# Where two subtractions that split x into bf16 parts are issued: on GpSimd between its gathers, or on VectorE around the first keys

## The reference

```
def _mp_layer(x, src, dst, edge_attr, W, b):
    # self loops with a zero attribute are appended: src2, dst2, ea2
    msg = concat([x[dst2], x[src2], ea2], axis=1) @ W + b
    agg = segment_sum(msg, dst2, num_segments=n)
    return relu(agg)

h   = relu(_mp_layer(x, src, dst, edge_attr, W1, b1))       # 64 -> 128
out = log_softmax(_mp_layer(h, src, dst, edge_attr, W2, b2))  # 128 -> 64
x   = layernorm(x + out)
```

## Time and profile before

| | us |
|---|---|
| median of three executions (251.25 to 252.3) | 251.34 |
| span of the profiled execution, first to last instruction | 251.8 |
| busy PE | 202.7 (81%), 2089 matmuls |
| busy PEld | 183.9 (73%) |
| busy DVE | 180.2 (72%), 436 instructions |
| busy POOL | 165.0 (66%), 338 instructions |
| busy ACT | 115.1 (46%), 235 instructions |
| chain of waits that ended last | PE 42%, POOL 34%, DVE 12%, DMA 5%, issue 4%, ACT 1% |
| mean granted TensorE clock | 0.972 of full |

### The profile page before, as it was taken

How to read it: one execution, slowest core, us unless ns; L and a number is a source line. 1 busy time by engine, 2 the same in 40 slices (tenths; PEclk the granted TensorE clock), 3 DMA queues, 4 the chain that set the end, 5 groups by cost and what they waited for, 6 DMA issues and landing times.

```text
span 251.8 us, 5544 instructions
## 1 busy us (share of the span) xinstructions
PE 202.7 (81%) x2089; PEld 183.9 (73%) x2089; DVE 180.2 (72%) x436; ACT 115.1 (46%) x235; POOL 165.0 (66%) x338
## 2 busy tenths in 40 slices
PE   1001269599998999989999899989999999999940
PEld 0000159489887898879888798878888999999930
DVE  4035999979876899768977789768410285899881
ACT  2020173267766676757766776667741010101110
POOL 5728998619999999999999999999846000000000
PEclk9999999779999999999999999999999999999995
DMA  1543200000000000000000000000000001010000
GB/s 35 136 115 85 63 21 21 0 3 1 3 2 3 0 3 3 1 3 1 3 1 3 0 3 0 4 0 5 0 3 0 3 3 31 3 31 23 19 15 18
DMA packets 12578, 4.18 MB, mean 17 GB/s; under 512 B 11911, under 2 KB 12126, under 8 KB 12551
## 3 DMA queue, kind: packets, MB, share of 16 engines
q1 hardware_dynamic: 10711, 1.77, 4.0%
q0 software_dynamic: 1840, 2.04, 3.0%
HBM read 2.98 MB, written 0.81 MB: 15 GB/s over the span
## 4 chain that ended last, share of the span: by engine, by line
PE 42%; POOL 34%; DVE 12%; DMA 5%; issue 4%; ACT 1%; POOLq 0%; ACTq 0%; DVEq 0%
PE pset L834 21%; PE acc L826 9%; PE pset L801 5%; POOL u L378 4%; POOL deg L377 4%; DMA adj<-in_dst,adj 4%; POOL t L390 3%; DVE ohl L504 3%; POOL t L394 3%; POOL z L389 3%; POOL u L381 3%; POOL zr L392 3%; POOL base L400 2%; POOL z L398 2%; POOL z L396 2%
## 5 line engine op out<-in xcount | busy, mean ns | idle before, releaser
L715 ACT ACTIVATE adj<-pset 125x1000 bf16<-125x1000 f32 x75 | 77.3, 1032 | 7.0 <-PE pset L801 7.0
L826 PE MATMUL acc<-x,adj 125*125 125x195 bf16 x625 | 75.7, 260 | 2.2 <-POOL x L329 2.2
L504 DVE TENSOR_TENSOR ohl<-iota,keyl 128x1000 bf16<-128x1000 bf16 (+1 forms) x75 | 60.0, 800 | 12.6 <-PE dense L814 11.8
L801 PE MATMUL pset<-ohr,ohl 128*125 128x125 bf16 x600 | 60.0, 255 | 6.0 <-DVE ohr L504 6.0
L826 PEld LDWEIGHTS acc<-x,adj 125*125 125x125 bf16 x625 | 59.7, 143 | 5.7 <-POOL x L329 2.4
L504 DVE TENSOR_TENSOR ohr<-iota,keyr 128x1000 bf16<-128x1000 bf16 (+1 forms) x75 | 60.7, 810 | 0.0
L801 PEld LDWEIGHTS pset<-ohr,ohl 128*125 128x125 bf16 x600 | 50.8, 154 | 7.9 <-DVE ohr L504 6.3
L834 PE MATMUL pset<-z,adj 125*125 125x192 bf16 x625 | 52.8, 247 | 0.0
L834 PEld LDWEIGHTS pset<-z,adj 125*125 125x125 bf16 x625 | 51.7, 136 | 0.3
L529 DVE TENSOR_REDUCE s_sum<-acc 125x65 f32<-125x195 f32 x25 | 9.1, 363 | 19.1 <-PE acc L826 18.7
L751 ACT ACTIVATE x<-x 125x192 f32<-125x192 f32 (+2 forms) x6 | 2.6, 427 | 38.5 <-DVE x L586 38.5
(11 more groups left out here) (114 smaller groups left out, 271.0 us busy)
## 6 DMA issues: line engine op xcount, KB each, us to landing
x_nat<-in_x SPq DMA_DIRECT2D x1, 781.2 KB
out<-x SPq DMA_DIRECT2D x2, 187.5 KB
out<-x SPq DMA_DIRECT2D x3, 93.8 KB
out<-x SPq DMA_DIRECT2D x1, 125.0 KB
adj<-in_dst,adj POOLq DMA_INDIRECT x5, 7.1
adj<-in_edges,adj POOLq DMA_INDIRECT x5, 4.0
adj<-in_edge_attr,adj POOLq DMA_INDIRECT x5, 3.5
se_scratch<-adj SPq DMA_DIRECT2D x5, 2.4 KB
```

Of the source, the lines that this page charges most:

```text
L504: ins = dve.tensor_tensor(out=oh[s][:, :, :, :], in0=iota2[:, 0:Q, :].unsqueeze(1).broadcast_to([128, n, Q, 2]), in1=key[:, g, k0:k0 + 2 * ...
L715: act.activation(adj4[0:Q, g, :, w0:w0 + 8 * WD].rearrange("p h (b e) -> p b h e", b=2), pset[s][0:Q, :, 0:4 * WD * G].rearrange("p b (h e ...
L801: ins = pe.matmul(pset[s][0:Q, i // 4, 0:4 * WD * G].rearrange("p (h e) -> p h e", h=G)[:, :, i % 4 * WD:(i % 4 + 1) * WD], ohl[s][:, i // ...
L826: ins = pe.matmul(acc[0:Q, 0:XW], adj4[0:Q, g, h, :], x3[:, h, :], start=(h == 0), stop=(h == G - 1))
```

## The change

The two POOL instructions are taken out of POOL's queue, so that POOL issues the attribute gathers 1 to 4 right behind the edge gathers. The same two subtractions, on the same tiles and with the same semaphores, are issued by DVE: the first between offset 3 and the keys of part 0, the second between offset 4 and the first one-hots. On ACT the rounding of part 1 goes ahead of the copies of the first keys.

```
@@ GpSimd
-            gp.wait_ge(xs_ready, 1)
-            gp.tensor_tensor(x_rest, x_nat[:, :, :], x3[:, :, 0:C], ALU.subtract).then_inc(xs_rest, 1)
-            for j in range(1, 3):
-                gather_attrs(j)
-
-            gp.wait_ge(xs_ready, 2)
-            gp.tensor_tensor(x3[:, :, 2 * XC:2 * XC + C], x_rest, x3[:, :, XC:XC + C], ALU.subtract).then_inc(xs_ready, 1)
-            for j in range(3, J):
+            for j in range(1, J):
                 gather_attrs(j)
@@ VectorE
+            dve.wait_ge(xs_ready, 1)
+            dve.tensor_tensor(x_rest, x_nat[:, :, :], x3[:, :, 0:C], ALU.subtract).then_inc(xs_rest, 1)
             keys(0, 1)
             offset(J - 1)
+            dve.wait_ge(xs_ready, 2)
+            dve.tensor_tensor(x3[:, :, 2 * XC:2 * XC + C], x_rest, x3[:, :, XC:XC + C], ALU.subtract).then_inc(xs_ready, 1)
             dve.wait_ge(consts, 11)
             dve.wait_ge(keys_ready, 1)
@@ ScalarE
+            act.wait_ge(xs_rest, 1)
+            act.activation(x3[:, :, XC:XC + C], x_rest, ACT.Copy).then_inc(xs_ready, 1)
             act.wait_ge(keyt_done, 1)
             copy_keys(keyl, acc[:, 0:Q], 0, 5)
             copy_keys(keyr, acc[:, Q:2 * Q], 0, 5).then_inc(keys_ready, 1)
-            act.wait_ge(xs_rest, 1)
-            act.activation(x3[:, :, XC:XC + C], x_rest, ACT.Copy).then_inc(xs_ready, 1)
```

## The result

The changed kernel takes 245.75 us (median of four executions, 245.49 to 246.47) against 251.82 us for the kernel before in the same session: the ratio is 0.9767, 95% interval 0.974 to 0.9793, so 2.3% faster, 6.07 us. Predicted were 245.2 and 6.1 us. In a second session both were timed again: 246.13 us (245.38 to 246.88, five executions) against 251.34, ratio 0.9783 (0.9762 to 0.9804), 5.2 us.

A forecast was written before the change was run, and what follows sets the result against it. DVE's chain up to the last key, held twice by POOL's subtractions, was taken to bound when the loop begins. -7.11 + 1.0 + 0.0 = -6.1 us, from the median 251.34 to 245.2 us; range 242.8 to 247.6.

The forecast's parts named there:

- The hold: DVE's one-hots stand still during POOL's two subtractions; removing these gains 3.62 + 3.49 = 7.11 us on DVE's chain.
- The two subtractions on DVE: Each occupies DVE for 1.75 us; the first fills a wait, the second delays the first one-hot by 1.0 us.
- POOL's queue: Attribute gathers end at about 34.9 us, L341 comes at 39.5; nothing is late, cost 0.0.
- The rule on who holds whom: Two-input DVE and SBUF-reading GpSimd instructions exclude each other, the later blocking; if gathers counted as reads, 2.4 us worse, 247.6.
- the mild reading: On POOL's gathers beside DVE's subtractions: descriptor generation needs only the write side, so neither is stretched.
- PE keeps up: Before the loop: layer 1 group 0 ends at 38.7, PE still waits 1.4 us for the key, 6.1 us passed on.
- Rival A: PE's clock around the loop's start: staying up gives 243.7 us, chance 0.13; slow for longer gives 246.7, chance 0.10.
- Rivals C and D: POOL's gathers hold DVE's one-hots instead, 252.7 us, chance 0.03; the stalls have another cause and stay, 252.3, chance 0.01.
- The accounting: Took the profiled span of 251.8 us as 0.46 above the runs' median and applied the difference to the median, 251.34.

The follow-up runs named there:

- first_only: Changed kernel with the second subtraction moved back from DVE to GpSimd, behind attribute gathers 1 and 2; 248.92 us.
- pool_read: Changed kernel plus one GpSimd subtraction of 125x1600 elements, its result unread, where the first subtraction stood; 249.04 us.
- pool_write: Changed kernel plus two GpSimd memsets, which only write SBUF, where the first subtraction stood; 251.04 us.
- layer1_late: Changed kernel in which PE waits also for attribute gather 2 ahead of the first layer-1 product; 245.81 us.
- before_again: The kernel before, unedited, profiled a second time; span 251.9 us, that execution 253.9 us.
- warm: Changed kernel plus 36 extra matmuls, results unread, in PE's wait for the last key; 246.16 us.

## Why the prediction was right

**The hold (7.11 us), right.** Both stretched one-hots are gone, and first_only and pool_read bring one back by putting a POOL subtraction back, at 3.90 and 4.30 us. DVE's stretch from first one-hot to last key took 14.10 us (24.64 to 38.74); 21.22 - 7.11 is 14.11. That it agrees to the hundredth is luck: in the second profiles the stretch takes 21.57 and 13.84 us, 7.7 apart, of which the two holds are 7.23. The term itself rests on rows of both profiles and on the two experiments.

**The two subtractions on DVE (1.75 us each, 1.0 in all), right in size, a little low in the sum.** They take 1.82 us each, and the next instruction begins 1.73 after, against 1.75 from the slope of two smaller shapes. The first is free. The first one-hot, counted from the first offset, comes after 10.38 us (10.15 in the second profile) instead of 9.16 (8.70): 1.2 to 1.5 us later where I had 1.0. Reckoned in the same way the last key is 5.9 us earlier (6.3 in the second pair), and with 0.44 us from the lap between the first and second reduction (6.66 instead of 7.10) the whole is 6.34 us in the first pair of profiles; the medians say 6.07 and 5.2. The 0.44 us is scatter of that lap, not a gain of the change: the two profiles of the kernel before differ in it by 1.36.

**POOL's queue, wrong, and right in its figures by luck.** The gathers ended at 34.90 as reckoned and L334 came at 39.53 against 39.5. But these figures were counted in a trace whose first row came 1.60 us later. Counted from the first offset, the gathers end after 20.64 us where 19.0 was reckoned, because one took 2.26 us beside DVE's first subtraction and others up to 1.73, and L334 starts after 25.27 where 23.6 was reckoned, because the attribute sums took 6.12 us (33.41 to 39.53) to go out and come back instead of 4.69. I wrote that nothing was late and priced no loss there. It was 1.6 us late, and that fitted into POOL's slack; pool_write shows that 3.0 us more on that queue cost 5.3 us, so the slack was small.

**The rule on who holds whom.** The extra GpSimd subtraction held DVE and the memsets did not, which is what the Trainium skill, page "SBUF — State Buffer", section "Who interferes with whom", says of GpSimd instructions that read and that only write. Its inference that a tensor_tensor leaves descriptor generation alone does not agree with these traces: the gather that starts at 18.59, beside the subtraction of 17.95 to 19.77, takes 2.26 us instead of 1.20 and ends 1.08 after it. I had taken the mild reading, and it was wrong for an instruction this long; the count of 0.66 us beside a gather that started in the same moment could not show it. It cost no time that shows: POOL had the 1.1 us to give, and DVE's subtractions took 1.82 us each time, beside a gather or not. The other half of the rule as I put it, that the later one waits for the first, is not what the rows show either: each held instruction on DVE started 0.46 to 0.60 us ahead of POOL's subtraction (27.06 and 27.66, 33.89 and 34.35, 29.14 and 29.61, 31.15 and 31.75) and was held all the same. Why the earlier one lost is open.

**PE keeps up, right, with a term mis-sized on the safe side.** Layer 1 starts 16.76 us behind the first offset, and 32.6 in the prediction is 16.7 behind it. But its first group then took 3.5 us (31.02 to 34.56) instead of the 6.14 taken from before, so PE's slack ahead of the last key was 4.23 us (3.27 in the second profile) and not 1.4. Part of the difference is PE's pace: eight build matmuls take 0.73 us from 31.8 on, where in the kernel before they take 1.21 at 39.02 and 1.20 at 41.49; the profile's granted clock reads 1.00 in both places, so only the durations show it. What a later layer 1 would cost at an equal clock no run shows, since in layer1_late the clock gave the delay back.

**Rival A, the clock, priced about right for one lap, and not a matter of this change.** In the first pair of profiles the slow stretch moved with everything (0.50 at 46.6 to 53.5 before, 37.7 to 44.5 now) and the laps across it take 7.10 and 6.66 us. In before_again, with 1.00 throughout, the same lap takes 5.74, 1.4 less than in the first profile of the same kernel. But in all three profiles with a first lap of 5.74 us (before_again, warm, first_only) the next one is longer, 8.47, 8.47 and 6.97 instead of 5.47, so the gain was taken back; pool_read (5.87, then 5.46) and layer1_late (6.21, then 5.46) show that it need not be. Warm kept the clock up and gained nothing in the median. Rivals C and D are out: the edge gather and four attribute gathers of POOL beside twelve one-hots cost the one-hots nothing, and the hold belongs to POOL's reading instruction. A gather seems to hold another kind of DVE instruction, though: the tensor_scalar of the keys at 20.34 takes 0.53 instead of 0.23 us and ends 0.02 behind the gather of 18.59, and one in the first profile of before takes 0.61 (22.31) and ends 0.03 behind a gather (21.69 to 22.89), so this is no cost of the change. No run tests it.

**The accounting** of span and median was wrong (0.46 us, where the profiled execution was some 2 us above the median) and did no harm, since only a difference was applied.

## What to carry to other kernels

When an instruction takes several times its normal duration, look at what ran beside it on the other engines, before looking at semaphores: here a 3.1 us GpSimd instruction that nobody on DVE waited for cost DVE 3.6 us. Moving such work onto the engine that was held cost less here than the hold, because it ran faster there (1.82 against 3.14 us), and less still where it fell into that engine's existing waits, which can mean moving its producer forward on a third engine (2.0 to 2.4 us here) or splitting its input (another 0.5 to 1.5). Compare times of two traces only from a common event: the absolute times of POOL's queue agreed with the forecast to a few hundredths of a us, and were 1.6 us off.

## What was not expected

The first laps of the loop are unstable: the same kernel, or one edited by a fraction of a microsecond, takes 5.47 or 8.47 us from the second to the third reduction of acc. The rows suggest how, though no run tests it: in the long laps of before_again and warm the lap before had been a fast one (clock 1.00, 5.74 us), DVE issues its one-hots with hardly a gap, POOL's four short instructions for u take 3.63 us together beside them instead of 1.76, and PE waits 1.73 and 1.74 us for u. In first_only the wait is the same 1.73 us, the clock stays at 1.00 and the lap takes 6.97; in the other two the clock then falls to 0.50 and it takes 8.47. So of the 3.0 us, about half is POOL's lateness and half the clock. In pool_write an instruction of 0.20 us took 3.17. A gain ahead of such a place is safe only to within some 3 us in a single execution, so it has to be read from medians and from the trace up to that place.
